# Fetching the eighth chunk of every fourth group row by row from SyncE and ScalarE, in a kernel whose row gathers run on GpSimd

## The reference, cut to what matters

```python
# 12,500 nodes x 128 features, 212,500 edges sorted by dst; the last 12,500 of them are self loops before the sort
# layer 1 (relational): W[r] = sum_b w_comp[r, b] * weight[b]
msg = (x @ W[etype])[src]
x1  = layernorm(x + segment_sum(msg, dst) + h_bias)
# layer 2 (mean of the neighbours)
agg = segment_sum(x1[src], dst); deg = max(segment_sum(1, dst), 1)
out = layernorm(x1 + x1 @ W_self + b_self + (agg / deg) @ W_neigh)
```

## Time and profile before

| | |
|---|---|
| time of one execution, median of 3 runs (lowest, highest) | 3921.51 us (3912.53, 3926.23) |
| span of the profiled execution, first to last instruction | 3299.5 us |
| the profiled execution's own time | not among the numbers shown; the median less the span is 622.0 us |
| instructions in the span | 35,621 |
| first sweep, GpSimd's first wide gather to the first late one | about 257 to 2119 us of the span |
| late sweep | about 2119 to 3299 us |

### The profile page before, as it was taken

The page is one execution under the profiler, slowest core; times in us unless marked ns, Lnnn a source line. Parts: engine busy times, 40 slices in busy tenths (PEclk is TensorE's granted clock), DMA queues, the critical chain, the costliest instruction groups (busy, mean ns, idle before and its releaser), DMA issues.

```text
span 3299.5 us, 35621 instructions
## 1 busy us (share of the span) xinstructions
PE 2010.2 (61%) x12511; PEld 1948.2 (59%) x12511; DVE 1379.0 (42%) x3552; ACT 317.5 (10%) x572; POOL 2457.6 (74%) x2590
## 2 busy tenths in 40 slices
PE   1756677767766777767766777544454444445454
PEld 1756676767766777767766777544444444444444
DVE  5533333233323333333333333245656676666434
ACT  2110111011111111111111111100000000000001
POOL 7777777777777777777777777577777777777774
PEclk9877777777787777777777777655566666666666
DMA  2953444344444444444444443212222222222232
GB/s 76 306 159 106 126 123 122 109 122 122 124 122 121 122 121 121 120 122 122 124 122 120 118 118 110 84 53 63 62 62 63 63 72 63 72 63 72 74 94 68
DMA packets 256767, 346.87 MB, mean 105 GB/s; under 512 B 46902, under 2 KB 188735, under 8 KB 256584
## 3 DMA queue, kind: packets, MB, share of 16 engines
q0 software_dynamic: 106000, 265.39, 28.1%
q1 hardware_dynamic: 150584, 79.16, 8.2%
HBM read 313.37 MB, written 43.84 MB: 108 GB/s over the span
## 4 chain that ended last, share of the span: by engine, by line
POOL 68%; issue 22%; PE 4%; DMA 1%; DVE 1%; ACT 0%; POOLq 0%; DVEq 0%; SPq 0%; ACTq 0%
POOL rows L1370 38%; POOL rows L1384 26%; POOL rows L1366 4%; PE zps L1876 2%; DMA rows<-x_x_rows,src_t 1%; PE yps L1903 1%; PE yps L1888 1%; PE tps L1903 0%; PE zps L1998 0%; PE tps L1888 0%; DMA rows<-x_rows,picked_mem 0%; PE yps L1915 0%; ACT xout L1399 0%; DVE stats L1472 0%; DVE xout L1466 0%
## 5 line engine op out<-in xcount | busy, mean ns | idle before, releaser
L1370 POOL DMA_INDIRECT rows<-x_x_rows,src_t x1469 | 1393.1, 948 | 447.5 <-issue 443.3
L1876 PE MATMUL zps<-acc,rows 128*128 128x168 f32 x3322 | 792.9, 416 | 527.0 <-DMA rows<-x_x_rows,src_t 496.5
L1876 PEld LDWEIGHTS zps<-acc,rows 128*128 128x128 f32 x3322 | 737.4, 274 | 546.8 <-issue 527.4
L1384 POOL DMA_INDIRECT rows<-x_rows,picked_mem x725 | 690.3, 952 | 220.9 <-issue 220.6
L1998 PE MATMUL zps<-acc,rows 128*128 128x128 f32 x1450 | 305.6, 397 | 341.5 <-DMA rows<-x_rows,picked_mem 339.3
L1998 PEld LDWEIGHTS zps<-acc,rows 128*128 128x128 f32 x1450 | 287.1, 303 | 350.9 <-issue 326.8
L1584 DVE TENSOR_TENSOR acc<-acc,yps 128x63 f32 (+1 forms) x535 | 116.8, 218 | 770.7 <-PE yps L1903 685.7
L1562 DVE TENSOR_TENSOR acc<-oh,tps 128x1344 f32<-128x1344 f32 x208 | 323.2, 1554 | 142.1 <-PE tps L1867 119.3
L1423 ACT COPY acc<-zps 128x672 f32<-128x672 f32 x208 | 148.9, 717 | 1569.1 <-PE zps L1876 1569.1
L1584 DVE TENSOR_TENSOR acc<-acc,tps 128x63 f32 (+1 forms) x296 | 64.5, 218 | 423.5 <-PE tps L1903 379.0
L1384 POOL DMA_INDIRECT rows<-x_rows,src_t x192 | 182.0, 948 | 77.2 <-issue 58.2
(11 more groups left out here) (257 smaller groups left out, 1886.8 us busy)
## 6 DMA issues: line engine op xcount, KB each, us to landing
rows<-x_x_rows,src_t POOLq DMA_INDIRECT x1469, 2.7
acc<-in_edge_type_dram SPq DMA_DIRECT2D x207, 64.0 KB
rows<-x_rows,picked_mem POOLq DMA_INDIRECT x725, 2.5
x_x_rows<-in_x_dram SPq DMA_DIRECT2D x20, 576.0 KB
x_x_rows<-zrow SPq DMA_DIRECT2D x20, 576.0 KB
xin<-in_x_dram SPq DMA_DIRECT2D x24, 256.0 KB, 3.3
x_rows<-xout SPq DMA_DIRECT2D x24, 256.0 KB
out_dram<-xout SPq DMA_DIRECT2D x24, 256.0 KB
```

Source lines behind the costliest of these rows:

```text
L1370: gather = pool.indirect_dma_start(out=wide_rows[:, g % WIDE_SLOTS, c, :], out_offset=None, in_=table, in_offset=bass.IndirectOffsetOnAxis ...
L1384: pool.indirect_dma_start(out=rows[:, j % SLOTS, c, :], out_offset=None, in_=x1_rows[0:n_nodes, :], in_offset=bass.IndirectOffsetOnAxis(ap ...
L1876: last = nc.tensor.matmul(zwins[g % 2][:, c // HALF, c % HALF // 2], slot_rows(g, c), a[:, g % 4, c], start=(c % 2 == 0), stop=(c % 2 == 1 ...
```

## The change

SyncE and ScalarE take over gathers from GpSimd. In the first sweep the eighth chunk (`HAND_COL`) of groups 23, 27, ..., 203 (46 of them) is fetched "by hand": 128 DMAs of one row, each from a byte offset that was loaded into a register. Of every three such groups SyncE has two (31) and ScalarE one (15); SyncE issues 32 rows at a time, ScalarE 16. In the late sweep the eighth chunk of 28 late groups is fetched so (18 by SyncE, 10 by ScalarE). The index lists are made once: VectorE multiplies indices by the row size, TensorE transposes them (`turn_hands`), ScalarE keeps them as integers; the late lists come unit by unit. As these fetches are issued early, the edges of the hand chunks are tested against the threshold of 13 groups before (`HAND_LAG`). `store_x1` and most of `store_out` move from SyncE to ScalarE, and SyncE's load of x for the next quad moves three positions down its program. With the planner's new `late_of` the late sweep has 919 chunks, still in 116 groups. The diff below is cut; its last hunks are, in this order, of SyncE, GpSimd, ScalarE in the first sweep, ScalarE in the late sweep, and TensorE.

```diff
+HAND_COL = CPG - 1
+HAND_BUFS = 3
+HAND_EVERY = 4
+HAND_LAG = 13
+SP_ROWS = 32
+ACT_ROWS = 16
...
     def late_of(g):
-        return P * CPG * (16.0 / 17.0 - early_share * QUAD * front(g))
+        lagging = front(g) - hand_front(g) if g % HAND_EVERY == HAND_EVERY - 1 else 0
+        return P * (CPG * (16.0 / 17.0 - early_share * QUAD * front(g)) + early_share * QUAD * lagging)
...
+            hand_groups = range(PLAIN - 1, last_group - 3, HAND_EVERY)
+            act_hands = list(hand_groups[3::3])
+            sp_hands = [g for g in hand_groups if g not in act_hands]
...
+            for i, g in enumerate(sp_hands):
+                second = i and g - sp_hands[i - 1] == HAND_EVERY
+                for part, ahead in enumerate((-6, -5, -3, -2) if second else (-8, -7, -5, -4)):
+                    sp_at.setdefault(g + ahead, []).append((i, part))
...
+            def fetch_rows(engine, only, r0, many, indices, source, to, landed):
+                row = source.shape[1] * 4
+                to_bytes = to.bitcast(U8)
+                from_bytes = source.rearrange("n f -> (n f)").bitcast(U8)
+                _, starts = nc.values_load_multi_w_load_instructions(
+                    indices[0:1, r0:r0 + many], engines=only, min_val=0, max_val=(source.shape[0] - 1) * row,
...
+                for e in range(many):
+                    engine.dma_start(to_bytes[r0 + e:r0 + e + 1, :],
+                                     from_bytes[bass.ds(starts[e], row)].rearrange("(o f) -> o f", o=1)).then_inc(landed, 16)
+            def fetch_hand(engine, only, hands, i, part, many):
+                g = hands[i]
+                if part == 0:
+                    engine.wait_ge(hand_kept, 1)
+                    if i >= HAND_BUFS:
...
+                    if hand_front(g):
+                        k = hand_front(g) - 1
+                        engine.wait_ge(stored1[k % 2], stores(k))
...
+            sp_lates = [j for j in range(5, late_groups - 4, 6) if HAND_COL in late_chunks(j)]
+            act_lates = [j for j in range(8, 3 * late_groups // 4, 8) if HAND_COL in late_chunks(j)]
...
-                        if g in out_at:
-                            if out_at[g] + 2 < all_quads:
-                                load(n1, out_at[g] + 2, x_in, False)
-                            if out_at[g] == 0:
-                                sp.wait_ge(table_in, table_parts)
-                            store_x1(out_at[g])
+                        if g - 3 in out_at and out_at[g - 3] + 2 < all_quads:
+                            load(n1, out_at[g - 3] + 2, x_in, False)
+                        for i, part in sp_at.get(g, ()):
+                            fetch_hand(sp, SP_ONLY, sp_hands, i, part, SP_ROWS)
...
-                        real = real_chunks(g)
-                        for c in range(real):
+                        pooled = pooled_chunks(g)
+                        for c in pooled:
...
                         if g in staged_at:
                             stage_quad(staged_at[g])
                             roots_of(n1, staged_at[g])
                             normalise_quad(n1, staged_at[g])
+                            if staged_at[g] == 0:
+                                act.wait_ge(table_in, table_parts)
+                            store_x1(staged_at[g])
                         if g in cleared_at:
                             clear_quad(cleared_at[g])
+                        if g in act_at:
+                            fetch_hand(act, ACT_ONLY, act_hands, *act_at[g], ACT_ROWS)
...
+                    fetch_before("start")
                     for k in range(closing[0]):
                         keep_x1t(k)
+                        fetch_before((k, "kept"))
                         roots_of(n2, k)
                         normalise_quad(n2, k)
+                        store_out(k)
...
+                        fetch_before((k, "out"))
...
                         for c in range(real_chunks(g)):
+                            if by_hand(g, c):
+                                _, landed, count = hand_place(g)
+                                pe.wait_ge(landed, count)
```

More of the change, by code:

```diff
@@ L26 @@
 BF16 = mybir.dt.bfloat16
+U8 = mybir.dt.uint8
 DVE_ONLY = [mybir.EngineType.DVE]
+SP_ONLY = [mybir.EngineType.SP]
+ACT_ONLY = [mybir.EngineType.Activation]
 P = 128
@@ new lines, in gnn_kernel, with by_hand, hand_place @@
+            for i, g in enumerate(act_hands):
+                free = [e for e in range(max(g - 16, hand_turn_at + 1), g - 2) if e not in staged_at and e not in cleared_at and e not in act_at]
+                assert len(free) >= P // ACT_ROWS, g
+                for part, e in enumerate(free[-(P // ACT_ROWS):]):
+                    act_at[e] = (i, part)
+            def by_hand(g, c):
+                return c == HAND_COL and g in hand_groups
+            def hand_place(g):
+                if g in act_hands:
+                    i = act_hands.index(g)
+                    return act_ring[:, i % HAND_BUFS], act_in1[i % HAND_BUFS], 16 * P * (i // HAND_BUFS + 1)
+                i = sp_hands.index(g)
+                return hand[:, i % HAND_BUFS], hand_in1[i % HAND_BUFS], 16 * P * (i // HAND_BUFS + 1)
@@ new lines, in fetch_rows @@
+            def fetch_rows(engine, only, r0, many, indices, source, to, landed):
[4 more added lines that the diff above has]
+                    indices[0:1, r0:r0 + many], engines=only, min_val=0, max_val=(source.shape[0] - 1) * row,
+                    skip_runtime_bounds_check_because="the first byte of a source's row, in the half of the table for it")
+                for e in range(many):
+                    engine.dma_start(to_bytes[r0 + e:r0 + e + 1, :],
+                                     from_bytes[bass.ds(starts[e], row)].rearrange("(o f) -> o f", o=1)).then_inc(landed, 16)
@@ new lines, in fetch_hand @@
+            def fetch_hand(engine, only, hands, i, part, many):
[3 more added lines that the diff above has]
+                    if i >= HAND_BUFS:
+                        before = hands[i - HAND_BUFS]
+                        if narrow(before):
+                            engine.wait_ge(w1.z_done, before + 1)
+                        else:
+                            engine.wait_ge(rows_read, before - PLAIN + 1)
+                    if not narrow(g):
+                        engine.wait_ge(table_in, table_parts)
+                    if hand_front(g):
+                        k = hand_front(g) - 1
+                        engine.wait_ge(stored1[k % 2], stores(k))
+                indices = hand_i[g % P:g % P + 1, g // P, :]
+                buf, landed, _ = hand_place(g)
+                if narrow(g):
+                    fetch_rows(engine, only, part * many, many, indices, x_in, buf[:, 0:d], landed)
+                else:
+                    fetch_rows(engine, only, part * many, many, indices, table, buf, landed)
@@ L1099, in products_before, with pooled_chunks @@
+            def pooled_chunks(g):
+                return [c for c in range(real_chunks(g)) if not by_hand(g, c)]
             def products_before(g):
@@ L1170, in steps_before @@
                 return min(j, PLAIN) * (DUOS - 1) + late_steps
+            places_for = [("start", e * 3 // 4) for e in range((final_group(0) + 3) * 4 // 3)]
+            for k in range(last_quad - 2):
+                places_for += [((k, "kept"), final_group(k) + 5)]
+                idle = max(1, (final_group(k + 1) - final_group(k) - 2) * 4 // 3)
+                places_for += [((k, "out"), final_group(k) + 6 + e * 3 // 4) for e in range(idle)]
+            act_late_at = {}
+            at = len(places_for)
+            for i, j in reversed(list(enumerate(act_lates))):
+                for part in reversed(range(P // ACT_ROWS)):
+                    at = max(e for e in range(at) if places_for[e][1] <= j - 2)
+                    act_late_at.setdefault(places_for[at][0], []).insert(0, (i, part))
             closing = range(last_quad - 2, all_quads)
@@ L1595, in mark_early @@
                             g0 = etiles + c0 // CPG
-                            after(dve, marked, 1 + 2 * part)
+                            after(dve, marked, 1 + 3 * part)
                             nc.vector.tensor_tensor(
@@ L1845, in bank_free @@
                             pe.wait_ge(s_loopc, holder[1] + 1)
+                        elif holder and holder[0] == "hand":
+                            pe.wait_ge(hand_kept, 1)
                         elif holder:
@@ L1861, in turn_loops, with turn_hands @@
                         last.then_inc(s_loops, 1)
+                    def turn_hands():
+                        bank_free("hand", 0)
+                        pe.wait_ge(hand_shown, 3)
+                        for h in range(2):
+                            last = nc.tensor.transpose(hand_rows[:, h, :], hand_f[:, h * P:(h + 1) * P], ident[:, :])
+                        last.then_inc(hand_turned, 1)
                     def scale_by_relation(m):
```

174 lines of the change are left out of this document (144 added, 30 removed).

## The result

The changed kernel took 4761.01 us (4754.70 to 4767.49, 4 runs) against 3921.68 us for the kernel before, a ratio of 1.214 with a 95% interval of 1.212 to 1.216. I had forecast 3833 us. One thing has to be said first, since no number can be read without it: the kernel before has two times. Each of the six chips was met only once, so it is not shown whether the pace belongs to the chip or to a condition that it was in. Times are compared on one chip, unless it is said otherwise.

The account below looks back on a forecast made before the run. GpSimd's gathers were taken as the bound, 1.25 us each. Removing 90.2 us, less 2 us of friction, gave 88 us off 3921.5 (span 3299.5 plus 622.0): 3833 us, range 3815 to 3860 at 70%.

Parts of the forecast that it names:

- The base of the sum: Whole kernel: span of 3299.5 us plus 622.0 us around it, taken as unchanged, making 3921.5 us before the saving.
- rival 4: Time outside the span: its 622 us grow with the program's 28% more instructions, so 4005 us; chance 2%.
- What is removed: GpSimd's gathers: 57.6 us less in the first sweep and 32.6 us in the late one, together 90.2 us.
- The price of a row on SyncE: SyncE's one-row fetches: 0.33 us a row (0.27 to 0.55), 0.30 for the DMA and 0.03 for the register load.
- SyncE costs nothing on the path: SyncE in 12 first-sweep groups: busy 93 of GpSimd's 116.5 us; late sweep 42 of 58 us; no cost.
- Rival 1: SyncE's program in the first sweep becomes the beat, TensorE waiting for hand rows: 4086 us, slower; chance 15%.
- the lead of 50 us: SyncE's hand chunks issued about 5 groups ahead of use, subtracted from the stall in the first sweep.
- Rival 2: ScalarE's parts delay its copies, or TensorE meets late hand rows at the start; half lost, 3877 us; chance 7%.
- Rival 3: DMA transfers: single rows queue on one DMA engine, 422 us in 12 groups, total above 4000 us; chance 2%.
- cost nothing: ScalarE's parts of 16 rows: 5.3 us in a group's 9.7 us, behind a 0.72 us copy, delaying nothing.

Follow-up runs that it names:

- free_hands: Changed kernel with its 74 hand chunks fetched by nobody, the seventh chunk read twice instead: 3820.07 us on a slow chip (kernel before 3919.91).
- late_start: Changed kernel without hand chunks in groups 23, 27, 31 and 35: 3213.85 us on a quick chip (kernel before 3298.08), 4691.46 on a slow one (3919.91).
- sp_third: Changed kernel with SyncE keeping 16 first-sweep and 9 late hand chunks, ScalarE none: 4021.88 us on a slow chip (kernel before 3919.91).

## Why the prediction was wrong

**The base of the sum.** "I take the 622.0 us around it as they are" failed before anything else. Spans and times agree to 4 us in every later run, on either kind of chip. A difference of 19% between a span and a time was the sign that the rows were of another pace than the times, and rival 4 was a wrong reading of it.

**What is removed** was right in both places: 90 us in the sum, 100 us (free_hands, one execution) on a slow chip, and on quick ones 72 us net with 17 us of new waits.

**The price of a row on SyncE** is the term that was mis-sized. I took 0.33 us. It is 0.40 on quick chips, where the DMA and its gaps were about right (0.33 for 0.30) and the register load, my 1 us for 32 registers, is 2.2. On the slow chip it is 0.64 to 0.66, through pauses that no row of the trace before could show, and above my upper bound of 0.55.

**The sentence "SyncE costs nothing on the path"** held at 111 of 116.5 us on quick chips and failed on slow chips. Rival 1, at 15%, is what happened, with its place (TensorE's wait for hand rows) and its sign in the profile (SyncE's waits gone). Its size came out at 4086 since I priced the row at 0.49. With the slow chip's numbers, which are read from the result itself, so that this is an account and no forecast, the same working gives: GpSimd needs 93 x 1.253 us and 12 waits of 1.96 us (622 / 318, the mean of a group), 140 us; SyncE 173; 33 us too many, 15.3 times, is 505 us. In the late sweep of the slow trace 734 gathers took 1,400 us (3200 to 4600), so six groups with 46 gathers take 88 us, against 46 x 1.257 + 6 x 1.96 = 70; 18 times 18 is 324 us. 3832 + 505 + 324 = 4661 us of 4761; the lead of 50 us that I granted SyncE is not in it, and did not show.

**Rival 2**, the catching up at the start, is real: 17 us on quick chips, shown by late_start. On a slow chip the version without it took 4691 us against the changed kernel's 4761 on another, one execution, so its share there is not settled. **Rival 3** is out as a cause: on a quick chip 384 rows a round went through in about 116.5 us, and on a slow one the delay is in SyncE's stream before a row is issued, at register moves too. (On the quick chip ScalarE's 3,200 rows are 1,920 packets of 1,024 B, 1,280 of 512 B and 3,200 of 4 B, so a row was not split over several engines; which engine took it no view shows.) **ScalarE** "cost nothing" was right on quick chips (29 of 31 us gained), wrong on slow chips (149 us): I priced its parts against the copy of the next group in the first sweep, and left out the late sweep's copies of a quad, which stand behind up to 62 rows.

The ratio that I forecast, 3833 / 3921.5 = 0.977, is near the one of the quick chips (0.978), in part by luck: the 88 us come from a span of 3299.5 us, of which they are 2.7%, and 72 us were measured, with SyncE at 111 us where I had 93. The direction and the mechanism hold on quick chips; as a forecast of the time it was wrong, and so were the odds.

**Open:** what pauses the instruction streams on slow chips, and whether the pace stays with a chip. The delays end some 0.7 us or a multiple of it apart, but no run changed them. Most of sp_third's 131 us stays open too.

## What to carry to other kernels

Compare the span of a trace with the time before anything is summed; where they differ (they agreed to 4 us in every later run here), the rows and the time are of different conditions, and a margin read from the rows can shrink by more than that ratio: here the time rose by 19% and the price of SyncE's row by 65%, from 0.40 to 0.66 us. A helper engine that is to be kept 95% busy (111 of 116.5 us) to win 2% is a bad bet: its reserve, not the bound engine's saving, decides the sign. And here the engine that issued many short instructions was the one that the slower issue hit hardest: GpSimd's gather took the same time on both kinds of chip.

## What was unexpected of the hardware

On quick chips a one-row DMA with its address in a register costs SyncE 0.33 us and ScalarE likewise (16 rows in 5.3 us), and loading 32 registers takes 2.2 us. On slow chips the same instruction stream runs at this pace for a part and then at about twice the price (64 rows in 46.59 us, loads included, 0.73 us a row), with delays that end 0.7 us or a multiple apart. GpSimd pays 1.96 us a group on the mean at its semaphore waits, and the same kernel takes 19% longer, while a gather's own time is the same on both (948 ns on the quick chip, 947 on the slow one).
